# A transformer block with an xLSTM scan on one NeuronCore: TensorE's small steps merged, the state's product moved to another bank, the order redrawn

## The reference

```python
x = x + 0.5 * ffn(layernorm(x))       # FFN "1"
x = x + attn_block(layernorm(x))      # "A" (scan and projections), then "L" (gated MLP inside)
x = x + 0.5 * ffn(layernorm(x))       # FFN "2", same weights as "1"
# ffn: relu(x @ wi + b + lora of the winning expert of 8) @ wo + wo_b
# attn_block(z): h = rmsnorm(z); q, k, v = h @ wq, h @ wk, h @ wv; i = exp(clip(h @ wi)), f = sigmoid(h @ wf)
#   for each token, 16 heads of 16:  C = f*C + i * v k^T;  n = f*n + i*k
#                                    y = (C q) / max(|n . q|, 1)
#   z = z + y @ wo;  z = z + (silu(h2 @ w_gate) * (h2 @ w_up)) @ w_down
```

## Time and profile before

| | us |
|---|---|
| median of 3 runs (lowest to highest) | 939.15 (937.07 to 939.82) |
| the profiled execution, its own time | 939.06 |
| its span, first to last instruction | 936.9 |
| TensorE busy | 865.0 |
| VectorE busy | 627.0 |
| mean granted clock of TensorE | 0.98 |

### The profile page before, as it was taken

One profiled execution on the slowest core, in us unless ns is written; L12 is line 12 of the kernel. 1 busy time (PEld: TensorE's weight loads), 2 busy tenths in 40 slices (PEclk: granted clock), 3 DMA queues, 4 the chain that ended last, 5 costly groups with the idle time before them and its releaser, 6 DMA issues. The chain is left out here.

```text
span 936.9 us, 30800 instructions
## 1 busy us (share of the span) xinstructions
PE 865.0 (92%) x12744; PEld 823.7 (88%) x12744; DVE 627.0 (67%) x1502; ACT 359.0 (38%) x716; POOL 244.5 (26%) x234
## 2 busy tenths in 40 slices
PE   2958889999899998999899999999989989898998
PEld 2947869999799998999899998999979979898998
DVE  5445677585866858486676758677576787687642
ACT  4453152433533344243523436234343452233431
POOL 2013332320422313322322313332042234411110
PEclk9988999999999999999999999999999999999999
DMA  9105434212243202442133312431035035500000
GB/s 263 57 14 140 131 95 126 66 40 70 83 132 86 58 19 55 124 126 58 36 94 116 87 40 73 139 112 35 24 103 154 11 110 140 152 25 2 1 24 23
DMA packets 66313, 76.04 MB, mean 81 GB/s; under 512 B 12702, under 2 KB 48670, under 8 KB 66176
## 3 DMA queue, kind: packets, MB, share of 16 engines
q1 hardware_dynamic: 66176, 74.09, 28.2%
HBM read 56.75 MB, written 17.30 MB: 79 GB/s over the span
## 5 line engine op out<-in xcount | busy, mean ns | idle before, releaser
L644 ACT ACTIVATE r_h<-bank 128x512 fp32r<-128x512 f32 x128 | 76.5, 598 | 233.6 <-PE bank L1128 164.9
L1093 PE MATMUL bank<-xT_hi,wi_hi 128*128 128x256 f32 x512 | 148.1, 289 | 2.6 <-DVE r_l L836 1.8
L1093 PE MATMUL bank<-wo_hi,r_h 128*128 128x256 f32 x512 | 147.7, 288 | 1.1 <-DVE r_l L836 0.5
L1095 PE MATMUL bank<-xT_lo,wi_hi 128*128 128x256 f32 x512 | 144.1, 282 | 0.0
L1094 PE MATMUL bank<-xT_hi,wi_lo 128*128 128x256 f32 x512 | 144.1, 281 | 0.0
L1095 PE MATMUL bank<-wo_lo,r_h 128*128 128x256 f32 x512 | 143.7, 281 | 0.0
L1094 PE MATMUL bank<-wo_hi,r_l 128*128 128x256 f32 x512 | 143.7, 281 | 0.0
L836 DVE SCALAR_TENSOR_TENSOR r_l<-bank,r_h 128x512 fp32r<-128x512 f32 x128 | 87.9, 687 | 82.7 <-ACT r_h L644 82.1
L1093 PE MATMUL bank<-xT_hi,wgu_hi 128*128 128x256 f32 x352 | 103.1, 293 | 0.6 <-DVE gm L845 0.5
L1093 PEld LDWEIGHTS bank<-xT_hi,wi_hi 128*128 128x128 f32 x512 | 97.3, 190 | 5.0 <-DVE r_l L836 2.4
L1093 PEld LDWEIGHTS bank<-wo_hi,r_h 128*128 128x128 f32 x512 | 96.4, 188 | 3.9 <-issue 2.5
(11 more groups left out here) (157 smaller groups left out, 2143.9 us busy)
## 6 DMA issues: line engine op xcount, KB each, us to landing
dm<-f_scratch SPq DMA_DIRECT2D x128, 128.0 KB, 3.0
arena<-parts_scratch SPq DMA_DIRECT2D x96, 128.0 KB
arena<-parts_scratch SPq DMA_DIRECT2D x96, 64.0 KB
arena<-parts_scratch SPq DMA_DIRECT2D x32, 192.0 KB
x<-in_x SPq DMA_DIRECT2D x16, 256.0 KB, 3.0
parts_scratch<-pa SPq DMA_DIRECT2D x64, 64.0 KB
parts_scratch<-pb SPq DMA_DIRECT2D x64, 64.0 KB
parts_scratch<-pc SPq DMA_DIRECT2D x64, 64.0 KB
```

Source lines behind the costliest of these rows:

```text
L644: nc.scalar.activation(flat(r_h[:, n]), U[use % 2][:], ACT.Relu).then_inc(f_rh, 1)
L1093: nc.tensor.matmul(dst, lh, rh, start=first, stop=False, **more)
L1095: return nc.tensor.matmul(dst, lh, rl, start=False, stop=last, **more)
```

## The change

Four things are changed together.

1. A step of S makes both units' scores of a chunk; between them it waits, as before, for the product of the unit two back.
2. A step of M makes, in this order: the state's product of the *next* chunk (where the next one is in the same block), both units' mixes of this chunk, and the carry. The state's product is written into bank `M`, behind the 272 columns of the mixes, instead of bank `W`. The product of a block's first chunk is an M step of its own. So M has 40 steps instead of 96, S 32 instead of 64, Y 64 instead of 96.
3. VectorE's updates of the state, two steps a chunk, leave its flow Y and become a flow C. C waits for `a_c`, since it reads the bank that the M step writes, and the M step waits at its head for the updates (`a_at`) and for `y` of the chunk before (`a_y`).
4. The order strings of all five engines are new.

The diff, with TensorE's strings and the first lines of two others:

```diff
--- before.py
+++ after.py
@@ -91,45 +91,43 @@
...
     "PE": """
-        3G U G 5U V 2U V 2U 2V 4U V U V U 2V 2G 5U G U G 2U G U G 7U V 2U V 2U 2V 4U S U V S Y V 2U M 2V M 2S M 2Y M G 2S Y G 3U M 2U M U M Y S U S G 2Y M U G
-        M U G 2U G M Y M 4U Y 2U Y V 2U V M 2U 2V Y U Y 3U V 2U G 2V S G V 4U V 2U V Y U V U G U S M U G U V U G V U G V S 2M S 3U V 2U V 3U 2V 2U Y 2U V 3U V
-        G 2V G U Y U Y U M 3U M S U M G Y U Y M G Y 2S G U S M U M U G 4U Y V Y 3U V U 2M Y S 2V M U Y 2U Y 2U V S 2U G U 3V 2U G 3U V M U V 2U V S G Y M U G
...
-        5U 2V 2U V G U V G 4U V G U V U G U V U V 5U V U V U V U V 6U V U 3V""",
+        3G U G 5U V U V U V U V 4U V 3U 3V 2G 6U G U G U G U G 8U V U V U V M S U V 6U 2V U V S V M Y S Y G M G 3U Y 3U G Y U S M U Y G Y M U G U Y U G Y 3U V
+        5U V U V G V 2U G 2U V 2U V 2U 2V U G 2U S V 2U M V U V U G 2U G U V U G U 2V 4U V 4U V U 2V 2U G 3U V U V G V U V S M 3U Y 2U S U G M Y G U Y G U Y
+        2U G S 2U M U Y U V U Y U V 2U V M S V Y 3U Y 3U V U V G U V U V U G U M 2U V U V U V S M U G 2U G V U S G U Y V U G Y V 4U V U V 2U V U V 3U G 2U V G
+        V 3U 2V U M 3U Y U G M S Y U G U Y G M U G Y 8U V 3U Y 2V Y V 5U V G U S U V M 2V G 4U V U V U S U V U M U G U V Y G 2U G V U G S M V 3U Y U 2V 2U G
+        3U V G V 4U V U V 2U 2V Y 5U Y M G U S U Y G Y M G U Y U G 7U V U V U V Y V 6U V 2U 2V G S V 2U G 2U M 2U 2V U V U M S G U Y U G V U G S 2U V G V 3U V
+        U Y 3U 2V 2U G V 4U V 2U V G U 2V U M 2U Y 2U G S M U G Y U G Y M Y G 4U Y 3U V Y 2U V 3U V S V 4U V U G V 2U V U V U G U M 2U V S M 2U 2V U G Y 2U G
+        Y V U G S M U G V 2U V 4U V U V 3U V G V 3U V 3U V G 2V 2U Y 3U G U Y M S Y G 2U Y M G 3U G Y 4U Y V U V G 5U 2V U G U V 4U 2V U V U G U S M 3U V U 2V
+        U G 2U V 2U V S 2U V M 2U Y 2U S Y M G Y U G U G Y 2U S U G M U Y 5U V Y U S M 3U V Y M V U V Y U M S V 3U G U 2V S M U V G Y U Y 2U V 2U Y M S Y V U
+        V Y U Y M 2U 2Y U V U G 2V 2U G 3U V U V U V G 3U G U V G 2U G 2V 3U V 2U V G 2U V U V G 4U G V 3U 2V G V 6U V U V U V 2U V 5U V U 3V""",
     "DVE": """
-        2G H 3G 3H 2G 3H G H R 2H R 2H 2R H 3R G R 3H 2R H 3G 2H 3G R 2G R G R H 3R G 2R 2H R 2G R H 2R H G 2R 2H 2R D 3R D P R P Y R D G D Y 2R G Y G P Y G D
...
+        G H 3G H G 2H G 2H G H G 2H 2R 3H 2R H 2R 2H G 2H R H 2R H R 3G H 4G R G R G 4R G 2H R H R G R G R G R H R 2H R D 3R 2D R 2P R C 2R G R D R C D R P 2G
...
     "SP": """
-        H 7A F X F E C E A E A 4K E A E 2A 2K E K E K E 6A F E A K F X 2E 2A C K A K A K 2E A K E 2K E K 7A E A F K A K E F K E A E C O A K O X K A K E 2K 3E
...
+        H 6A X A F A E A F K E K E 2A K C 2E 2K A K 3E 2K 6A F E F X 2A C A E K A E 2K E K 2A E K E K E K 6A E K F A K 2A 2E K 2A E F C E O A K O X 2K E 2K 3E
...
@@ -1024,14 +1022,17 @@
                     v.tensor_tensor(pt[:, n % 2], S[n % 2][:], dm[:, n % DMBUFS], ALU.mult).then_inc(a_P, 1)
                     yield
 
-            def Y_():
+            def C_():
+
+                added = M[:, H * HV:H * HV + DC * 4 * HV].rearrange("p (c e m d) -> p c e m d", c=DC, e=2, m=2)
                 for b, j in chunks:
                     n = b * TILES + j
-
-                    added = W[:, 0:DC * 4 * HV].rearrange("p (c e m d) -> p c e m d", c=DC, e=2, m=2)
                     two = lambda t: t.rearrange("p (e d) -> p e d", e=2)
                     end = lambda c, m: cumE[:, c, j * P + m * TH + TH - 1:j * P + m * TH + TH]
                     dve.wait_ge(a_state, n + 1)
+                    if j:
+
+                        dve.wait_ge(a_c, n)
                     dve.wait_ge(a_ex[1], n)
                     if not opens(b, j):
                         dve.wait_ge(d_ce, 16 * DC * (b + 1))
@@ -1052,6 +1053,10 @@
                             v.scalar_tensor_tensor(two(c_at[0][:, c]), two(c_at[1][:, c]), end(c, 1), added[:, c, :, 1],
                                                    ALU.mult, ALU.add).then_inc(a_at[0], 1)
                         yield
+
+            def Y_():
+                for b, j in chunks:
+                    n = b * TILES + j
 
                     heads = M[:, 0:H * HV].rearrange("p (h m d) -> p h m d", m=2, d=HV)
                     sums = heads[:, :, :, HD]
@@ -1083,7 +1088,7 @@
                     v.bn_stats(z_st[:, j], z[:, j]).then_inc(a_zs, 1)
                     yield
 
-            merge("DVE", {"H": H_(), "R": R_(), "G": G_(), "D": D_(), "P": P_(), "Y": Y_()})
+            merge("DVE", {"H": H_(), "R": R_(), "G": G_(), "D": D_(), "P": P_(), "C": C_(), "Y": Y_()})
 
 
         @block.tensor
@@ -1275,11 +1280,10 @@
 
 
             def S_():
-                for b in range(BLOCKS):
-                    for u in range(UNITS):
-                        j, g = divmod(u, NG)
-                        n = UNITS * b + u
-                        pe.wait_ge(d_stack[j % 2], 16 * STACK_LOADS * (2 * b + j // 2 + 1))
+                for b, j in chunks:
+                    pe.wait_ge(d_stack[j % 2], 16 * STACK_LOADS * (2 * b + j // 2 + 1))
+                    for g in range(NG):
+                        n = UNITS * b + NG * j + g
                         if n > 1:
                             pe.wait_ge(a_P, n - 1)
                         for i in range(GH):
@@ -1290,65 +1294,73 @@
                                 done = nc.tensor.matmul(S[n % 2][tile, i * TH:(i + 1) * TH], ks[:, j % 2, h, tile], qs[:, j % 2, h, own],
                                                         start=True, stop=True)
                         done.then_inc(a_S, 1)
-                        yield
+                    yield
 
             def M_():
-                for b in range(BLOCKS):
-                    for u in range(UNITS):
-                        j, g = divmod(u, NG)
-                        n = UNITS * b + u
-                        pe.wait_ge(a_P, n + 1)
-                        if g == 0:
-                            pe.wait_ge(f_read, a_use(b, A_V + j // 2) + 1)
-                            if TILES * b + j:
-                                pe.wait_ge(a_y, TILES * b + j)
-
+                def state(b, j):
+
+                    pe.wait_ge(a_wv, NG * (TILES * b + j + 1))
+                    for c in range(DC):
+                        for q in range(COLS):
+                            tile = slice(q * P // COLS, (q + 1) * P // COLS)
+                            of = c * P + q * P // COLS
+                            done = nc.tensor.matmul(M[tile, H * HV + c * 4 * HV:H * HV + (c + 1) * 4 * HV], k32[:, b % 2, j, of:of + P // COLS],
+                                                    wv[:, HH * c + 2 * q:HH * c + 2 * q + 2].rearrange("p h m d -> p (h m d)"),
+                                                    start=True, stop=True)
+                    done.then_inc(a_state, 1)
+
+                heads = M[:, 0:H * HV].rearrange("p (h m d) -> p h m d", m=2, d=HV)
+                for b, j in chunks:
+                    n = TILES * b + j
+                    if j == 0:
+
+                        if n:
+                            pe.wait_ge(a_y, n)
+                            pe.wait_ge(a_at[1], DC * n)
+                            pe.wait_ge(a_at[0], DC * n_on(*chunks[n - 1]))
+                        state(b, j)
+                        yield
+
+                    pe.wait_ge(a_at[1], DC * (n + 1))
+                    pe.wait_ge(a_at[0], DC * n_on(b, j))
+                    if n:
+                        pe.wait_ge(a_y, n)
+                    if j < TILES - 1:
+                        state(b, j + 1)
+                    pe.wait_ge(f_read, a_use(b, A_V + j // 2) + 1)
+
+                    for g in range(NG):
+                        u = NG * n + g
+                        pe.wait_ge(a_P, u + 1)
                         for i in range(GH // 2):
                             pair = GH // 2 * g + i
                             for q in range(COLS):
                                 tile = slice(q * P // COLS, (q + 1) * P // COLS)
                                 of = (2 * i + q // 2) * TH + q % 2 * (P // COLS)
-                                done = nc.tensor.matmul(M[tile, pair * 2 * HV:(pair + 1) * 2 * HV], pt[:, n % 2, of:of + P // COLS],
+                                done = nc.tensor.matmul(M[tile, pair * 2 * HV:(pair + 1) * 2 * HV], pt[:, u % 2, of:of + P // COLS],
                                                         values(b, j)[:, 2 * pair + q // 2].rearrange("p m d -> p (m d)"),
                                                         start=pair == 0, stop=False, skip_group_check=True)
                         done.then_inc(a_O, 1)
-                        yield
-                        if g < NG - 1:
-                            continue
-                        c_n = TILES * b + j
-                        pe.wait_ge(a_ex[1], c_n + 1)
-                        pe.wait_ge(a_qc, DC * (b + 1))
-                        if not opens(b, j):
-                            pe.wait_ge(a_ex[0], n_on(*chunks[c_n - 1]))
```

(63 more changed lines are left out.)

27 lines of the change are left out of this document (2 added, 25 removed).

## The result

| | before | after |
|---|---|---|
| median, us (lowest to highest) | 938.11 (935.75 to 939.82, 4 runs) | 944.57 (943.71 to 948.02, 4 runs) |
| profiled span, us | 936.9 | 941.7 |
| TensorE busy, us | 865.0 | 853.4 |
| TensorE idle, us | 71.9 | 88.3 |

The change makes the kernel slower: ratio 1.01, 95% interval 1.0063 to 1.0137, 6.5 us by the medians. The forecast was 926.5 with a range of 914 to 940. The first term mostly came true: TensorE's busy time fell by 11.6 us. But its idle time rose by 16.4. The granted clock isn't the cause: 0.982 in the mean of the profiled execution after, 0.980 before.

What follows compares the result with a forecast made beforehand. TensorE, busy 92% of the span, was taken to bound the kernel. From 939.1 us, 14.7 for fewer trips and 2.9 for waits on `z` came off and 5 of new waits came on: 926.5 us, range 914 to 940.

Steps and rivals of the forecast that it cites:

- The first term: TensorE's order: 49 fewer trips from big products to small column tiles and back, 0.30 us each, 14.7 us saved.
- Fewer trips: TensorE's small steps merged, 114 stretches to 65, saving 49 switches from big products to small tiles and back: 14.7 us.
- I find no way in which this term is a loss: Said of merging TensorE's small steps: 14.7 us gained, 9.3 at the low end, the number of matmuls unchanged.
- the other terms: TensorE's waits in the scan: 2.9 us for `z` saved, about 5 us of new waits at M steps' heads.
- The state inside the M step: Next chunk's state product heading the M step: 2.9 us of waits go, about 5 new, most at chunk 1.
- The `z` wait: TensorE's wait ahead of the state's product (L1345), on a bank shared with `y`'s transposes: 2.9 us, to go.
- The rest: VectorE's separate flow C and the other engines' redrawn order: nothing net, give or take 6 us steady, 4 at start.
- Rival A: The M step as a lockstep: late decay-matrix loads in SP's in-order queue hold TensorE; 944 us; chance 0.14.
- Rival B: Merging TensorE's small steps saves nothing, slow ends stay inside merged steps; no change, 935 to 939 us; chance 0.12.
- C: Rival: the order is also better, TensorE's steady idle time falls by a third, fewer 1.2 GHz spells; 913 us; chance 0.09.

Runs made afterwards that it cites:

- wide pair: The changed kernel and the kernel before, each with two 64-column tiles for four 32-column tiles in scores, mixes and carry: 926.90 us and 939.86 us.
- scores-wide pair: The changed kernel and the kernel before, each with two 64-column tiles in the scores only: 925.37 us and 936.06 us.

## Why the prediction was wrong, point by point

*Fewer trips: right in kind, mis-sized.* 14.7 us forecast; measured 11.6 (after), 12.7 (wide pair) and 11.4 (scores-wide pair) of busy time, 0.23 to 0.26 us a trip instead of 0.30. The rows after the change show where the rest stays: 64 scores take 0.69 us to the next start (301.65 to 302.34), not the 0.48 of two that stand in company. The rule of the Trainium skill on instruction overhead (TensorEngine Tiling (Array Packing), Instruction Overhead), by which merging would save nothing, did not hold here: merging saved 11.4 to 12.7 us.

*"I find no way in which this term is a loss": this sentence failed.* The prediction counted that the number of matmuls is the same and looked no further. The same instructions in fewer, denser stretches outrun the fetch: 15.9 us of new issue waits, more than the 11.6 saved. Without the fetch the total comes out, 13.0 us measured on the wide pair against 12.6 forecast, but in part by luck: the trips brought 2.0 us less than forecast, and idle time fell by 1.8 us where the other terms (2.9 saved, 5 new) have it rise by 2.1.

*The state inside the M step: too large, and in another place.* 2.0 us of waits ahead of L1307 instead of 5, and none at chunk 1, where most of them was forecast: 0.4 us in the step of chunk 10, for `wv`, and 1.6 us in that of chunk 25, for `c_at`. The `z` wait went, as said. The waits for `y` grew by 4.0 us, which the sum did not have: M steps end together with the whole chunk, and `y`'s transposes stand right behind them (the longest 2.6 us, at chunk 0).

*The rest, "nothing net": right within 4 us.* In the wide pair, idle time is 1.8 us lower instead of 2.1 higher.

*Rival A* had nearly the right time, 944, by the wrong mechanism: 0.4 us of waits for `wv`. A number that agrees says nothing of the cause. *Rival B* fell with the busy time, and *C* did not occur: idle time rose.

What could be seen in advance: the unnamed issue waits in the profile of before, at borders of 256, and the count of instructions in a merged pair of steps. The price of such a border, 3.5 to 4 us a block, was nowhere in the rows of before by itself.

## What to carry to other kernels

Merging small TensorE steps saves the trips between big products and small column tiles, some 0.25 us each here, but count the instructions as well: a stretch that uses up 256 of them (weight loads, matmuls, waits) in less than 3.5 to 4 us can end in a wait. This is no sharp limit. After the change, 9 of the 13 blocks used up in less than 4.0 us ended in a wait, and so did 6 blocks that took 4.0 to 6.2 us and whose packet had started late, 1.5 to 3.6 us after the border instead of 1.0. Waits that name no engine are worth the question whether they stand at a fixed distance in the instruction stream; a few dozen to a hundred small instructions in front show it, if what they cost themselves is read from the trace. Where a step is dense, first look for wider tiles that do the same work in fewer instructions: on the scores this was free, and it turned a change with a ratio of 1.01 into one with 0.9875.

## What the runs showed of the hardware

- TensorE's instructions come in blocks of 256 (packets of 16 KB on q8) while the kernel runs. Back to back, a block takes 3.5 to 4.0 us, and 4.6 to 6.2 us beside the input loads. TensorE goes on 1.2 us or more after the end of the packet, 1.2 to 1.6 us where it had to wait for it.
- The place of a block's border, in the changed kernel with 0 to 192 instructions in front, moved the sum of fetch waits between 9.7 and 22.2 us and the median by 12 us of 940 (the ratio to before from 1.01 to 0.9951).
- Two 64-column tiles instead of four 32-column tiles: free for scores (96 rows, bf16, 64 columns streamed), but 0.17 to 0.20 us dearer a unit for the float32 mixes (34 columns streamed).
